# Edges' target terms of a graph attention layer: stationary one-hots against stationary terms

## The reference, cut to what matters

```
ft = layernorm(x) @ W                       # 4 heads of 64
e  = leaky(e_src[src] + e_dst[dst])         # per edge and head; e_src, e_dst: sums of ft * attention weights
ex = exp(e - segment_max(e, dst)[dst])
out = segment_sum(ft[src] * ex / segment_sum(ex, dst)[dst] * dist, dst)
x1 = x + out
y  = x1 + sum_e softmax(ln(x1) @ Wr + br)[e] * expert_e(ln(x1))    # three 256 x 256 layers each
```

## Time and profile before

| | us |
|---|---|
| runs, median of 3 | 1558.58 (1556.54 to 1559.61) |
| profiled execution: span from first to last instruction (the page gives no other time of it) | 1556.4 |
| TensorE busy | 1485.0 (95%) |
| VectorE busy | 1231.7 (79%) |
| GpSimd busy | 1063.0 (68%) |
| ScalarE busy | 742.2 (48%) |

### The profile page before, as it was taken

How to read it: one execution, slowest core, us unless ns; L and a number is a source line. 1 busy time by engine, 2 the same in 40 slices (tenths; PEclk the granted TensorE clock), 3 DMA queues, 4 the chain that set the end, 5 groups by cost and what they waited for, 6 DMA issues and landing times.

```text
span 1556.4 us, 24165 instructions
## 1 busy us (share of the span) xinstructions
PE 1485.0 (95%) x8478; PEld 1298.3 (83%) x8478; DVE 1231.7 (79%) x2302; ACT 742.2 (48%) x1293; POOL 1063.0 (68%) x951
## 2 busy tenths in 40 slices
PE   6928999999999999999999999999999999999998
PEld 4727888878888888888888888888888888888887
DVE  7746787887788888878888888888888888888751
ACT  3500444444455555545555555554555555555543
POOL 4176767777778777777777877777777787787000
PEclk9959999999999999999999999999999999999999
DMA  8776344353543444353344444434334444443000
GB/s 239 203 233 192 110 137 124 106 141 94 144 121 111 122 126 127 103 142 108 103 135 118 112 119 118 128 106 137 108 107 134 119 111 119 129 111 91 18 7 8
DMA packets 106070, 187.50 MB, mean 120 GB/s; under 512 B 38357, under 2 KB 70490, under 8 KB 105919
## 3 DMA queue, kind: packets, MB, share of 16 engines
q0 software_dynamic: 44688, 123.13, 28.5%
q1 hardware_dynamic: 60701, 62.29, 13.9%
q10 hardware_dynamic: 560, 0.52, 0.1%
HBM read 172.72 MB, written 14.42 MB: 120 GB/s over the span
## 4 chain that ended last, share of the span: by engine, by line
PE 82%; DVE 9%; DMA 3%; issue 2%; ACT 2%; POOL 1%; SPq 0%; DVEq 0%; ACTq 0%
PE bankH L831 39%; PE bankY L860 21%; PE bankE L783 5%; PE bankE L784 5%; PE bankB L761 3%; PE bankE L776 2%; DVE gath L1431 1%; POOL gath L675 1%; DVE msg_lo L1437 1%; ACT h L1030 1%; DMA table<-gath 1%; PE bankA L808 1%; DVE x L1506 1%; DMA gath<-table,src_win 1%; PE bankA L799 1%
## 5 line engine op out<-in xcount | busy, mean ns | idle before, releaser
L675 POOL DMA_INDIRECT gath<-table,src_win x900 | 1042.5, 1158 | 336.0 <-issue 245.2
L1030 ACT ACTIVATE h<-bankH,bn_shift,bn_scale 128x250 f32<-128x250 f32 x800 | 400.9, 552 | 314.9 <-PE bankH L831 314.7
L831 PE MATMUL bankH<-h,w 128*128 128x250 f32 x1600 | 380.5, 380 | 2.8 <-ACT h L1030 2.1
L860 PE MATMUL bankY<-wo,h 128*125 128x256 f32 x1600 | 378.4, 379 | 1.1 <-DVE x L1506 1.1
L831 PE MATMUL bankH<-xT,w 128*128 128x250 f32 x1600 | 370.9, 374 | 0.3 <-ACT h L1030 0.3
L860 PEld LDWEIGHTS bankY<-wo,h 128*125 128x125 f32 x1600 | 296.1, 187 | 43.2 <-issue 1.4
L831 PEld LDWEIGHTS bankH<-h,w 128*128 128x128 f32 x1600 | 295.6, 191 | 43.4 <-issue 9.6
L831 PEld LDWEIGHTS bankH<-xT,w 128*128 128x128 f32 x1600 | 296.7, 190 | 32.2 <-ACT h L1030 0.4
L1437 DVE TENSOR_TENSOR msg_lo<-gath,msg_hi 128x2340 fp32r<-128x2340 f32 x90 | 234.3, 2603 | 88.0 <-ACT msg_hi L1002 88.0
L1002 ACT ACTIVATE msg_hi<-gath 128x2340 fp32r<-128x2340 f32 x90 | 193.8, 2154 | 217.0 <-PE bankE L784 192.0
L1506 DVE SCALAR_TENSOR_TENSOR x<-bankY,gate,x 125x256 f32<-125x256 f32 x400 | 173.9, 476 | 116.7 <-PE bankY L860 116.1
(11 more groups left out here) (190 smaller groups left out, 1027.6 us busy)
## 6 DMA issues: line engine op xcount, KB each, us to landing
onehot_t<-dst_low SPq DMA_DIRECT2D x48, 576.0 KB, 5.9
gath<-table,src_win POOLq DMA_INDIRECT x900, 2.9
x_res<-in_x SPq DMA_DIRECT2D x25, 250.0 KB
out<-x SPq DMA_DIRECT2D x25, 250.0 KB
table<-gath SPq DMA_DIRECT2D x25, 227.5 KB
w<-in_L_ffn_W SPq DMA_DIRECT2D x8, 512.0 KB
gath<-in_x SPq DMA_DIRECT2D x5, 672.0 KB
wo<-in_L_ffn_Wo SPq DMA_DIRECT2D x4, 512.0 KB
```

Of the source, the lines that this page charges most:

```text
L675: pool.indirect_dma_start(gath[:, g.slot(u), t, :], None, table, bass.IndirectOffsetOnAxis(src_win[:, g.win, u, t:t + 1], 0)).then_inc(row ...
L831: mm = pe.matmul(target[:, hc * 2 * NT:(hc + 1) * 2 * NT], weights[:, e * KC + c, hc * P:(hc + 1) * P], operand(c), start=(c == 0), stop=( ...
L860: mm = pe.matmul(bankY[0:NT, u * D:(u + 1) * D], h2[:, e % 2, c, u, :], wo[:, e * KC + c, :], start=(c == 0), stop=(c == KC - 1))
L1030: ins = act.activation(target[:, e % 2, hc, :, :].rearrange("p u n -> p (u n)"), source[:, hc * 2 * NT:(hc + 1) * 2 * NT], ACT.Relu, bias= ...
```

## The change

The roles in `to_edges` are turned round: the weights are a tile's 12 parts, and the one-hot streams, in eight pieces of 288 edges, four of them to separate output partitions 0, 32, 64 and 96. Two rounds (r) accumulate into one bank: a zero block beside the parts puts the second round's result 12 partitions higher. The two tiles go to steps 3 and 4. ACT copies the result out of `bankB`, SP stores it to DRAM in 8 transfers and reads it back in the edges' layout, and VectorE sums the parts from that. The residual's x goes straight into `x1`, whose buffer is that of the pair stored last. In the diff PH is 12 (3 parts by 4 heads), EC is 288 and GROUPS is 4. Not shown are: TensorE's and ACT's bodies, which call `to_edges` and `keep_edges` (behind `keep_bounds`) for tile 0 in step 3 and tile 1 in step 4, and TensorE's `first`, which calls it for all four tiles of pairs 0 and 1; `residual`, which now writes the quotient to `xn` and adds x1 to it, without the wait for `out_stored`; and `edge_parts`, which writes a tile's three parts side by side, every second block of 12 left zero.

```diff
-        edst_parts = sb("edst_parts", [P, PARTS, TILES * H], BF16)
+        edst_parts = sb("edst_parts", [P, 2 * TILES + 1, PH], BF16)
+        ed_rows = sb("ed_rows", [P, EC])
+        ed_parts = sb("ed_parts", [P, 2, PH, TE])
-        x_first = x_res
+        x_first = w1[:, 0:RING * 2, :].rearrange("p (g u) d -> p g u d", g=RING)
...
             def load_weights():
+                sp.wait_ge(t_norm, RING * 2)
...
             def load_res(g):
-                sp.dma_start(x_res[0:NT, g.par, :, :], x_pairs[g.n]).then_inc(x_in[g.par], 16)
+                if g.begins(2):
+                    sp.wait_ge(t_turned, NP)
+                else:
+                    sp.wait_ge(out_stored[g.par], g.half * 16)
+                sp.dma_start(x1[0:NT, g.par, :, :], x_pairs[g.n]).then_inc(x_in[g.par], 16)
...
+            def store_edges(a, u):
+                sp.wait_ge(ed_kept, a.tile(u) + 1)
+                rows = edge_rows[a.tile(u) % EDGE_RING].rearrange("q (r j c) -> j r q c", r=2, j=GROUPS)
+                for j in range(GROUPS):
+                    for r in range(2):
+                        sp.dma_start(rows[j, r], ed_rows[32 * j + r * PH:32 * j + (r + 1) * PH, :]).then_inc(ed_stored, 16)
+
+            def load_edges(a, u):
+                sp.wait_ge(ed_stored, (a.tile(u) + 1) * 2 * GROUPS * 16)
+                if not a.begins(1):
+                    sp.wait_ge(ed_ready, a.n)
+                sp.dma_start(ed_parts[:, u, :, :], edge_rows[a.tile(u) % EDGE_RING].rearrange("q (p t) -> p q t", t=TE)).then_inc(ed_in[u], 16)
...
             def first(a):
                 load_dst_low(a + 1, 0)
+                store_edges(a, 0)
                 load_dst_low(a + 1, 1)
+                store_edges(a, 1)
+                for u in range(2):
+                    load_edges(a, u)
+                for u in range(2):
+                    store_edges(a + 1, u)
                 load_weights()
+                for u in range(2):
+                    load_edges(a + 1, u)
...
             def body(f, g, a):
                 if f is not None and not f.begins(1):
                     store(f + -1)
+                if g is not None and not g.begins(2):
+                    load_res(g)
+                for u in range(2):
+                    if a is not None and (a + 1).within(NP):
+                        load_dst_low(a + 1, u)
+                    if a is not None and f is not None:
+                        store_edges(a, u)
+                if a is not None and f is not None:
+                    for u in range(2):
+                        load_edges(a, u)
                 if g is not None and (g + WINS).within(NP):
                     sp.wait_ge(msg_ready, g.n * CHUNKS + (3 if len(plan_of(g).passes) > 1 else 1))
                     load_window(sp, g + WINS)
-                if a is not None and (a + 1).within(NP):
-                    load_dst_low(a + 1, 0)
-                if g is not None and (g + 2).within(NP):
-                    sp.wait_ge(xn_ready, g.n * 2 + 2)
-                    load_res(g + 2)
-                if a is not None and (a + 1).within(NP):
-                    load_dst_low(a + 1, 1)
...
-            def to_edges(a):
+            def to_edges(a, u):
+                if a.begins(1) and u == 0:
                     pe.wait_ge(parts_ready, 1)
                 else:
-                    pe.wait_ge(ed_ready, a.n)
+                    pe.wait_ge(ed_kept, a.tile(u))
+                pe.wait_ge(onehotT_ready, a.tile(u) + 1)
+                stacked = edst_parts[0:NT].rearrange("n b q -> n (b q)")
+                for r in range(2):
+                    cols = (a.tile(u) * 2 + 1 - r) * PH
+                    for j in range(GROUPS):
+                        at = (r * GROUPS + j) * EC
+                        mm = pe.matmul(bankB[32 * j:32 * j + 2 * PH, 0:EC], stacked[:, cols:cols + 2 * PH], onehot_t[0:NT, u, at:at + EC],
+                                       start=(r == 0), stop=(r == 1))
+                mm.then_inc(edge_done, 1)
...
+            def keep_edges(a, u):
+                act.wait_ge(edge_done, a.tile(u) + 1)
+                if not a.begins(1) or u:
+                    act.wait_ge(ed_stored, a.tile(u) * 2 * GROUPS * 16)
+                act.activation(ed_rows[0:120, :], bankB[0:120, 0:EC], ACT.Copy).then_inc(ed_kept, 1)
...
              def first(a):
                 keep_bounds(a)
+                for pair in (a, a + 1):
+                    for u in range(2):
+                        keep_edges(pair, u)
...
+            own.did(dve.memset(edst_parts[:], 0.0))
+            own.did(dve.memset(bankB[:, ROWX:EC], 0.0))
             def edge_sum(a):
-                dve.wait_ge(edge_done, a.n * 2 + 2)
-                dve.tensor_reduce(ed[:].rearrange("p s t -> p (s t)"),
-                                  bankB[:, 0:PARTS * SEG * TE].rearrange("p (k c) -> p c k", k=PARTS), AX.X, ALU.add).then_inc(ed_ready, 1)
+                for u in range(2):
+                    dve.wait_ge(ed_in[u], (a.n + 1) * 16)
+                dve.tensor_reduce(ed[:].rearrange("p (u h) t -> p u (h t)", u=2),
+                                  ed_parts[:].rearrange("p u (k h) t -> p u (h t) k", k=PARTS), AX.X, ALU.add).then_inc(ed_ready, 1)
```

More of the change, by code:

```diff
@@ L44 @@
 PARTS = 3
+PH = PARTS * H
+GROUPS = 4
+EC = WIN // (2 * GROUPS)
+EDGE_RING = 4
 X_GROUPS = (0, 1, 2, 4, 6, 9, 12, 15, 18, 21, 25)
@@ L87, with __init__ @@
 class Plan:
-    def __init__(self, sums, place=1, bounds=3, new=1, rows=3, onehots=None, residuals=None, products=None, passes=(), low=()):
+    def __init__(self, sums, place=1, bounds=3, new=1, rows=3, onehots=None, edges=(3, 4), residuals=None, products=None, passes=(), low=()):
+        self.edges = edges
         self.sums, self.place, self.bounds, self.new, self.rows, self.onehots = sums, place, bounds, new, rows, onehots
@@ L240, in gnn_ffn_kernel @@
         dist_win = sb("dist_win", [P, WINS, 2, TE])
-        x_res = sb("x_res", [P, RING, 2, D])
         bounds = sb("bounds", [P, 2, 2, H])
@@ L750, in turn_carry @@
                 mm.then_inc(carry_back, 1)
-            def to_edges(a):
-                if a.begins(1):
+            def to_edges(a, u):
+                if a.begins(1) and u == 0:
                     pe.wait_ge(parts_ready, 1)
                 else:
-                    pe.wait_ge(ed_ready, a.n)
-                for u in range(2):
-                    pe.wait_ge(onehotT_ready, a.tile(u) + 1)
-                    for t in range(TE):
-                        mm = pe.matmul(bankB[:, 0:PARTS * SEG * TE].rearrange("p (k s t) -> p k s t", k=PARTS, t=TE)[:, :, u * H:(u + 1) * H, t],
-                                       onehot_t[0:NT, u, t:WIN:TE], edst_parts[0:NT, :, a.tile(u) * H:(a.tile(u) + 1) * H],
-                                       start=True, stop=True)
-                        if t == TE - 1:
-                            mm.then_inc(edge_done, 1)
-                        yield
+                    pe.wait_ge(ed_kept, a.tile(u))
[8 more added lines that the diff above has]
+                mm.then_inc(edge_done, 1)
             def aggregate(g, c):
@@ L871, in first @@
                 for pair in (a, a + 1):
-                    for _ in to_edges(pair):
-                        pass
+                    for u in range(2):
+                        to_edges(pair, u)
             def body(f, g, a):
-                small = to_edges(a) if f is not None and a is not None else iter(())
                 plan = plan_of(g)
@@ L894, in body @@
                         turn_bounds(f, a)
-                        for _ in small:
-                            pass
+                    if f is not None and a is not None and s in plan.edges:
+                        to_edges(a, plan.edges.index(s))
                     if run and (s >= 1 or not f.begins(1)):
@@ L1060, in body @@
                         keep_bounds(a)
+                    if f is not None and a is not None and s in plan.edges:
+                        keep_edges(a, plan.edges.index(s))
                     if g is not None and s == max(plan.residuals):
@@ L1441, in residual @@
                 dve.wait_ge(agg_done, g.n * CHUNKS + 2 * u + 2)
-                dve.wait_ge(x_in[g.par], (g.half + 1) * 16)
+                if u == 0:
+                    dve.wait_ge(x_in[g.par], (g.half + 1) * 16)
                 own.did(dve.tensor_scalar(rden[0:NT, u, :], bankE[u][0:NT, D:ROW], TINY, None, ALU.max))
@@ L1446, in residual @@
                 own.settle()
-                if not g.begins(2):
-                    dve.wait_ge(out_stored[g.par], g.half * 16)
-                own.did(dve.tensor_tensor(x1[0:NT, g.par, u, :].rearrange("n (h c) -> n h c", h=H),
+                own.did(dve.tensor_tensor(xn[0:NT, u, :].rearrange("n (h c) -> n h c", h=H),
                                           bankE[u][0:NT, 0:D].rearrange("n (h c) -> n h c", h=H),
@@ L1452, in residual @@
                 own.settle()
```

(11 more changed lines are left out.)

5 lines of the change are left out of this document (4 added, 1 removed).

## The result

The changed kernel takes 1545.8 us (median of 4 runs, 1543.34 to 1550.04), the kernel before on the same chip 1559.09 (1556.54 to 1560.84): a ratio of 0.9912, 95% interval 0.9897 to 0.9927. The profiled spans are 1543.7 and 1556.4 us, 12.7 apart.

A forecast was written before the change was run, and what follows sets the result against it. TensorE, busy 55.53 of a steady stage's 55.60 us, was taken as the bound. Start +9.8 and pipeline -18.6 made -8.8 on the 1556.4 span, 1547.6; with 2.2 for the median, 1550 us (1541 to 1563; with rivals 1539 to 1578).

The forecast's parts named there:

- The forecast's course: Whole kernel: start loses 9.8 us, pipeline saves 18.6, giving 1550 us, 1541 to 1563; chance 0.60.
- the pipeline: Stages after the start: 18 steady ones save 0.91 us each, 5 early ones 0.45; 18.6 us saved (12 to 24).
- the start: Before the first expert: VectorE's sum waits for SP's stores and loads, and weights move later; 9.8 us lost (6 to 18).
- (A): Rival, TensorE: a tile's eight matmuls stream one after another, 1.31 us a tile; 1578 us; chance 0.21.
- (D): Rival, TensorE: each weight load waits for the matmul before it, 3.2 us a tile; 1665 us; chance 0.03.
- (B): Rival, step 3: TensorE waits at the aggregation for VectorE's later low_part, 0.5 us a stage kept; 1558.6 us; chance 0.10.
- (C): Rival, start: it costs nothing, as pieces land faster and gathers set the pace; 1540 us; chance 0.06.
- A tile: TensorE's cost for one tile's target terms, 0.40 us stream plus 0.25 weight-width change: 0.65 us (0.52 to 0.81).
- The early stages: Five pipeline stages before the even ones, with waits for gathers and VectorE: half the saving, 0.45 us each.
- The 2.5 us that the spreads of pair 2 were to give back: In the start's sum: pair 2's spreads, which made a later gather land in 5.38 us, come earlier; 2.5 us back.
- ACT's 1.3 us: At the start: ACT holds the exponential until the stores of pair 1's first tile are back, 1.3 us late.
- ACT's copies: Two copies of 288 columns a steady stage, about 0.6 us each: free, without a wait for transfers.

The follow-up runs named there:

- e1: The changed kernel with all eight matmuls of a tile writing one group's output partitions instead of four groups' (three quarters of the terms lost): 1582.93 us, ratio 1.0148.
- e2: The changed kernel with each tile's two rounds of four matmuls done twice, same result: 1557.6 us, ratio 0.9981.
- e7: e5 with ACT's copy of pair 1's second tile moved behind the exponentials of pair 0's first tile: 1531.63 us, ratio 0.9833.
- e5: e3's VectorE order, and SP at the start issues pair 0's small stores and loads ahead of spreads, last window and x: 1534.37 us, ratio 0.9834.
- e9: e7 with weights issued behind pair 1's spreads and x, ahead of the last window; pair 1's second copy after the second tile's exponentials: 1533.12 us, ratio 0.9833.
- e4: The changed kernel with SP issuing pair 0's stores and loads ahead of pair 1's two spreads at the start: 1543.7 us, ratio 0.9896.
- e3: The changed kernel with VectorE making pair 0's onehots and pair 1's transposed ones before pair 0's sum: 1538.92 us, ratio 0.9871.

## Why the prediction was right, and which of its terms were off

The forecast's course is what happened: four groups stream abreast, the pipeline gains, the start loses, the sum is in favour. The time lies inside the range of that course, and rivals (A) to (D) did not happen: (A) is e1, a real alternative that the groups' partitions rule out; against (B), the aggregation of step 3 starts at 862.54 behind layers without a gap, 0.27 us after `low_part` has ended (VectorE's row):

```profile
859.67 2.60 DVE L1489 TENSOR_TENSOR msg_lo<-gath,msg_hi 128x2340 fp32r<-128x2340 f32 x1 [1.06 <-ACT msg_hi L1046]
```

(C) falls with the start's loss, (D) with the 0.35 us. But three terms were mis-sized, in opposite directions: the pipeline gave 30.6 us instead of 18.6, the start took 17.9 instead of 9.8. That the time came within 5 us of the forecast is partly luck, errors of 12.0 and 8.1 that offset each other; with the start's error alone the forecast's sum would have been 17.9 - 18.6 = -0.7, a change that can't be told from none. In the sum itself one end was wrong: a start of 18 less a pipeline of 12 is +6, not +4, so this course reached to 1565.

**A tile: 0.65 us forecast, 0.43 measured**, below the given bounds of 0.52 to 0.81. The stream was taken as 0.40, a point between four abreast (0.27) and the issue rate of the old kernel (0.49); it is 0.24 (e2), the end of full overlap. The bound by issue was read from 36 pairs in 2.21 us, but those had loads of 128 columns; the new loads have 24, and eight of them took 0.11 us. A rate read from one shape was carried to another. The width change was 0.25 for one tile and is 0.19. A stage therefore saves 1.35, not 0.91. Of the 1.08 us to the next layer in e1, 0.97 are stream when the same 0.11 (0.35 - 0.24) is taken off, so four groups are four times as fast as one. The factor of 2.38 for three groups that the prediction cited from the Trainium skill ("TensorE: Matmul & The Clock Gate", Part 3) is 0.79 a group, less than the 1.0 a group that these runs show for four.

**The early stages: half of a stage's saving forecast, 2.3 in all, 6.28 measured.** Five full savings would be 6.75. The 2.5 us that the spreads of pair 2 were to give back stood in the start's sum, but 14.24 and 3.74 make up all of the start, and behind the first expert they did not come either. VectorE's `runs` for which the gather of 5.38 landed, and its next wait for a gather in the changed kernel:

```profile
159.18 0.22 DVE L1366 COPY logit<-gath 128x72 f32<-128x72 f32 x1 [0.17 <-DMA gath<-table,src_win]
```

```profile
203.79 0.22 DVE L1417 COPY logit<-gath 128x72 f32<-128x72 f32 x1 [6.97 <-DMA gath<-table,src_win]
```

Before, VectorE waited only 0.17 us for that gather; in the changed kernel these `runs` stand 5.96 us behind the first expert instead of 6.23. The next ones wait 6.97 us instead of 2.64, and the second target terms of the pipeline (250.36, before 230.52) are 1.91 further behind the first expert than before. The four stages from there to the even ones then gain 8.19, where four full savings are 5.40; where the other 2.8 come from is open. They are not the late start caught up: in e7 the first expert comes 14.35 us earlier than in the change, and the same stretch takes 307.97 against 307.96.

**The start: 9.8 us forecast, 17.93 measured** (12.3 forecast without the spreads' 2.5; 1.04 of the 17.93 are the scatter ahead of the first target terms). The step that failed is "8 stores to 97.9, spread for tile 1 at 98.7, 8 stores to 102.5". It treats the second eight stores as ready. They wait for a copy on ACT, the copy for the first eight stores' landing, and these for the spread ahead of them. The prediction knew this wait and priced it in the steady stage and for pair 1, and left it out of pair 0, where it is worst. Measured: second stores issued at 107.42 instead of 99.1. From there on its terms hold: landing 1.72 (2.2 forecast), the loads 2.73 (3.0), the work behind the sum 6.96 (7.3), the gather 3.74 (3.1). ACT's 1.3 us were not lost in the changed kernel (the exponentials stand 14.25 later, the `runs` 14.24); they surfaced as soon as the sum was early, in e5.

**The edits costed at nothing.** ACT's copies take 0.41 us (0.6). In the steady stage shown the waits view has this line, a wait of 0.9 us that the forecast did not have; TensorE is busy 54.10 of the 54.25 us all the same:

```profile
ACT ed_rows L1039 <- DMA edge_rows<-ed_rows: 0.9, 1, 0.9
```
For `load_res` and `residual` the steady stage is the evidence: two tiles at the 0.45 us read in step 4 leave 1.31 of the old 2.21, and the stage saved 1.35, so hardly anything is left for them to have cost. The x part was not tried by itself.

**The signs.** A tile above 0.87 us or a first expert past 171 was to prove it wrong. The first expert came at 170.88, at the edge; it was the pipeline's larger saving, not the start, that kept the sign. ACT's copies were to have no wait for transfers; they have the one above.

## What to carry to other kernels

Here an intermediate that goes over DRAM in small pieces cost nothing that could be read in the steady pipeline, with a stage of slack, and most of the 17.9 us where the pipeline is filled: sum that place alone, in the order of each queue, and give every buffer that is written again its wait. In a queue, put small transfers that someone waits for ahead of large ones that nobody waits for yet (here 1.7 us against 6.4 to 8.6), and on an engine put work that needs nothing ahead of the instruction that waits. With both, and ACT's copy moved by the same rule, the start's loss fell from 17.9 to 3.6 us (16.9 to 2.9 from the first target terms), and e7 and e9, at a ratio of 0.9833, beat the kernel before and the change.

## What the runs showed of the hardware that was not expected

Four matmuls into four groups of 32 output partitions, each with 125 input rows, run in the time of one: 0.12 us a round of 288 columns (e2). Loads of 24 columns cost 0.11 us for eight, and change of width 0.19 us a tile. Store transfers of 13.5 KB land in 1.7 us when nothing large is just ahead in their queue (1.4 to 2.5 in the same place in e1 to e4), in 6.2 to 6.4 behind 500 KB of x (e5, e4), in 8.56 behind a spread and the x loads (8.2 to 10.3 in e1 to e3); in a queue of their own under the weights in 4.7 to 4.9.
